# Causal attention with routed experts on one core: the expert units are laid out over fewer of the attention slots

## The reference

```
xn  = layernorm(x)
out = x + attention(xn) + experts(xn)

attention: q, k, v = xn@Wq+bq, xn@Wk+bk, xn@Wv+bv     16 heads of 16
           softmax(q k^T / 4, causal) v, then @ Wo + bo
experts:   16 routed experts, 4 per token, inner width 176, softmax gate, weights renormalised
           y = sum of weight * (silu(x Wg) * (x Wu)) Wd
           and a shared expert of inner width 352 for every token
```

## Time and profile before

| | |
|---|---|
| median of 3 runs | 1187.9 us (1186.93 to 1193.66) |
| the profiled execution's own time | 1184.47 us |
| its span, first to last instruction | 1182.9 us |
| mean granted TensorE clock | 0.939 of full |
| busy: PE, DVE, ACT, POOL | 989.0, 855.2, 652.1, 586.8 us |
| slots 0 to 319 (first to last exponential's start) | 204.1 to 1138.0 us |
| from there to the end | 44.9 us |

### The profile page before, as it was taken

The page is one execution under the profiler, slowest core; times in us unless marked ns, Lnnn a source line. Parts: engine busy times, 40 slices in busy tenths (PEclk is TensorE's granted clock), DMA queues, the critical chain, the costliest instruction groups (busy, mean ns, idle before and its releaser), DMA issues.

```text
span 1182.9 us, 26391 instructions
## 1 busy us (share of the span) xinstructions
PE 989.0 (84%) x8630; PEld 519.4 (44%) x8630; DVE 855.2 (72%) x1787; ACT 652.1 (55%) x1219; POOL 586.8 (50%) x527
## 2 busy tenths in 40 slices
PE   2877515999989899989998999999889998999980
PEld 1454302544444444544444445444444554444450
DVE  5888687888888877667876676777777767786320
ACT  4777500554545455466665654666656556766630
POOL 6433207777761004356665653566556535667521
PEclk9888755999999999999998999999999999999995
DMA  6998726223233313544454443644444445444348
GB/s 168 282 294 279 238 64 179 70 71 99 71 109 104 92 55 78 91 83 91 87 96 83 83 83 66 106 91 90 91 86 88 86 74 98 67 78 71 67 68 152
DMA packets 102284, 128.01 MB, mean 108 GB/s; under 512 B 25513, under 2 KB 86202, under 8 KB 101650
## 3 DMA queue, kind: packets, MB, share of 16 engines
q0 software_dynamic: 41632, 60.79, 28.6%
q1 hardware_dynamic: 60530, 65.59, 18.8%
HBM read 72.16 MB, written 57.82 MB: 110 GB/s over the span
## 4 chain that ended last, share of the span: by engine, by line
PE 55%; DVE 13%; issue 7%; ACT 4%; DMA 3%; SPq 1%; POOL 0%; ACTq 0%; DVEq 0%; POOLq 0%
PE gup L1191 12%; PE pvp L1131 11%; PE outs L1218 9%; DVE part L1285 7%; PE smp L1087 6%; PE turn L1203 5%; PE stp L1112 4%; PE outs L1138 4%; PE turn L1167 3%; DVE sg L1324 2%; PE smp L1070 1%; ACT XC L1440 1%; DVE hf L1329 1%; ACT th L1429 1%; DVE probs L1357 1%
## 5 line engine op out<-in xcount | busy, mean ns | idle before, releaser
L1423 ACT ACTIVATE probs<-stp 128x1024 f32<-128x1024 f32 (+1 forms) x320 | 300.4, 939 | 276.0 <-PE stp L1112 271.2
L1285 DVE TENSOR_REDUCE part<-smp 128x2 f32<-128x256 f32 (+2 forms) x372 | 345.8, 951 | 45.3 <-PE smp L1070 28.2
L1191 PE MATMUL gup<-gu_w,XC 128*128 (+1 forms) x1248 | 226.4, 318 | 11.3 <-DVE hf L1329 10.8
L934 POOL DMA_INDIRECT XG<-xrow_d,slots x144 | 146.5, 1017 | 131.6 <-DMA out<-Y 86.3
L941 POOL DMA_INDIRECT out<-Y,slots x72 | 118.1, 1640 | 136.1 <-ACT Y L1456 113.9
L1218 PE MATMUL outs<-dn_w,h 88*128 (+1 forms) x1248 | 181.0, 276 | 0.1
L941 POOL DMA_INDIRECT acc_d<-Y,slots x72 | 118.8, 1650 | 118.6 <-ACT Y L1456 104.9
L1131 PE MATMUL pvp<-probs,Vs 128*32 128x512 f32 (+3 forms) x1536 | 165.5, 503 | 3.3 <-DVE probs L1357 2.7
L1324 DVE SCALAR_TENSOR_TENSOR sg<-th,gup 128x176 f32<-128x176 f32 x208 | 69.8, 336 | 119.9 <-ACT th L1429 117.4
L1087 PE MATMUL smp<-Ks,Qs 48*128 48x128 f16 (+2 forms) x744 | 112.3, 340 | 45.7 <-DVE part L1285 26.9
L923 POOL DMA_INDIRECT slot_d<-entry,slot_i x128 | 128.5, 1004 | 42.8 <-issue 42.8
(11 more groups left out here) (168 smaller groups left out, 1099.2 us busy)
## 6 DMA issues: line engine op xcount, KB each, us to landing
rb<-rsum_d SPq DMA_DIRECT2D x64, 128.0 KB
Ks<-k_d SPq DMA_DIRECT2D x96, 64.0 KB
Qs<-q_d SPq DMA_DIRECT2D x96, 64.0 KB
v_d<-V SPq DMA_DIRECT2D x8, 544.0 KB, 4.6
Vs<-v_d SPq DMA_DIRECT2D x16, 272.0 KB, 3.3
acc_d<-YA SPq DMA_DIRECT2D x1, 4224.0 KB, 16.3
X<-L_attn_x POOLq DMA_DIRECT2D x8, 512.0 KB, 4.7
xrow_d<-XR SPq DMA_DIRECT2D x8, 512.0 KB, 5.0
```

What stands on the lines that cost most here:

```text
L934: pool.indirect_dma_start(XG[:, q].rearrange("p a c t -> p (a c t)"), None, s.xrow_d, bass.IndirectOffsetOnAxis(ap=slots[:, r, 0:1], axis= ...
L1191: last = pe.matmul(gup[:, 0:2 * I], XC[:, x % 2, a, h], weights_of(s.gu_w, e, b, h, slice(0, 2 * I)), start=n == 0, stop=n == 5)
L1285: last = dve.tensor_reduce(part[:, g % 2, k0 // CH, :, j, t], banks[:, :, col:col + w], AX.X, ALU.max)
L1423: act.activation(to, of, ACT.Exp, scale=float(DK) ** -0.5 / QS ** 2).then_inc(exp_done, 1)
```

## The change

`SPARE` goes from 4 to 18: the planner divides the same work by 302 slots instead of 316.

```diff
-        LAG, SPARE = 2, 4
+        LAG, SPARE = 2, 18
         FIRST, SECOND = spread_units()
         second_slot = {v: g * SLOTS + n for (g, n), v in SECOND.items()}
```

## The result

The changed kernel takes 1208.7 us (median of 6 runs, 1205.02 to 1212.81) against 1185.5 us (6 runs) of the kernel before: ratio 1.0193, 95% interval 1.0172 to 1.0215, or +23 us (+20 to +25). The forecast was 1201, +13. The direction and the range held; the loss is nearly twice the forecast's. The profiled execution has a span of 1203.4 us, 20.5 more than the one before; it was the fastest of its six.

The account below looks back on a forecast made before the run. PE was taken to bound the kernel, busy 989.0 us. +33 us in the first 296 slots less 20 at the end gave +13 on a median of 1187.9, so 1201 us, range 1186 to 1211.

Parts of the forecast that it names:

- Part 1: End of the kernel: last scatter and merges stay behind the last down product after slot 319; cost and gain 0.
- Rival 4: End of the kernel: the merges start early, beside the attention, some 25 us of the end go, 1176; chance 0.03.
- Part 2: Slot 296 to the start of slot 319, emptied of units: from 64.4 to 40.7 us at full clock, gain 24.
- Part 3: Emptied stretch from slot 296: PE about half busy, clock falls to 1.2 GHz for a good part, +4 (0 to +12).
- The swing: Emptied stretch: PE's share rises again at half clock and the next window was faster, so +4, a third of 12.
- rival 1: Stretch without units stays at 1.2 GHz, costing 12 us there: +21 in all, or 1209; chance 0.18.
- Part 4: First 296 slots take the 35 us of moved PE work, 2 us of it hidden: +33 (bounds +18 and +37).
- rivals 2 and 3: Slots 0 to 295: PE's idles hide half the moved work (1186, chance 0.13) or nearly all (1176, chance 0.11).

Follow-up runs that it names:

- experiment 3: Changed kernel with the last unit's down product and result issued behind its second half: ratio to before 1.0157; kernel before with them in slot 316: 0.9988.
- experiment 1: Kernel before (SPARE 4) with the last 14 of the 144 routed units left out altogether: ratio 0.9897, 12 us faster.

## Why the forecast came out as it did, step by step

- **Part 1, the end does not move by the layout: right.** POOL waited 49.2 us for the last unit, and the tail was 43.5 us against 44.9. From the last down product to the end it was 41.8 us (from 1161.60) against 42.8; the forecast said 43. Rival 4 is out, and experiment 3 shows that this order is the reason: with the last unit early the tail is 29.4 us.
- **Part 2, the emptied stretch at full clock: right.** The forecast said 40.7 us; with the clock held up (0.96) it took 41.5. One count was off: 16 second halves leave slots 296 to 319, not 15. A slip without effect: in group 14 DVE has 13.8 us free (58.0 less 44.2), not 14 or more.
- **Part 3, the clock: mechanism right, size off.** The term was +4; it measured 6.4 (47.9 less 41.5). PE's share did rise at the lower clock, to 26.3 of 38.0 us in the last group, but the clock stayed at 0.54. The swing that I drew from the earlier trace rows did not come; the row from 176 us there, low clock at 58% busy, was the better guide. This is half of rival 1: its condition held, but its price of 12 was too high. By the Trainium skill's rule on swinging ("TensorE: Matmul & The Clock Gate", "A second HAM failure mode: psum-queue depth-cycling") the term was +6, near the measured one. The trace shows little swinging, though: in windows of 3 us from 1119 to 1140 the clock was 0.96 once (from 1134) and 0.50 to 0.61 in all others, and from 1140 to 1160 it was 0.50.
- **Part 4, the price ahead of slot 296: right in kind, too small.** The term was +33, with a bound of +37; the profile has +38.8. PE's busy time there rose by 841.8 less 804.7 = 37.1 us and its idle from 64.8 to 66.5. So nothing of the moved work hid in the idles, the 2 us that I had let hide included; rivals 2 and 3 are out. Of the 37.1 us, 1.1 is the second half that I missed, and up to 2.7 are not moved work at all but a lower clock: slots 0 to 295 lost 12.6 us of full clock to its falls instead of 9.9. What the moved work itself takes is then near the 35 us. Part 4 had no term for the clock.
- **The sum.** Forecast +33 less 20 = +13. Profile +38.8 less 16.5, 1.4 and 0.4 = +20.5. Runs +23. The two mis-sized terms were Part 4 (5.8 us) and Part 3 (2.4 us), and both erred towards the small side. The measured 1208.7 us is rival 1's number, 1209, but that is luck: the clock in the emptied stretch was half of what rival 1 charged, and the rest lies ahead of slot 296.
- **What the forecast did not have.** Its Part 4 prices moved work by its amount alone. The ratios of SPARE 1 and SPARE 11 show that this is not enough: a step the other way costs 13 us instead of gaining 2 to 5, and half of the way costs three quarters of the loss. In the profiles the first 296 slots are off by several us (SPARE 1: 9.6 us longer with some 7 us less work), with different falls of the clock and different waits; which of the two is the cause is open. That the amounts fit so well for 18 may be partly luck, and the 35 us between the changed kernel and experiment 1 may contain such a share too.

## What to carry to other kernels

Before work is moved away from the end so that the end comes earlier, look which instruction releases the last transfer: here the last unit's result stood behind the loop in program order, and no layout could move it. Where one engine is busy for nine tenths of the time, ask whether what is taken from a looser stretch is paid in full in the dense ones, as the 35 us were here, and whether the loose stretch gives back as much as it lost: here it gave back 16.5 us for the 35, and 6.4 us of what is missing was its clock. Before a large transfer is moved beside other work, look whether small transfers are due then that an engine waits for. And a price per slot did not carry from one value of a layout's constant to the next here: 1 and 11 both came out slower than it said, so each value has to be measured.

## What the runs showed of the hardware that was not expected

- PE at 0.54 of full clock for 38 us while it was busy for 26.3 of them; with products added that nobody reads the stretch went from 47.9 to 41.5 us and the kernel from 1.0193 to 1.0101.
- Beside merges of 1024 KB, which kept the DMA engines busy (share 0.91 to 1.02, 207 to 213 GB/s), a write of 16 KB took 9.4 us instead of 1.4.
- A wait of PE of 2 us was followed by 6 us at a mean clock of 0.72 in one place and 0.50 in another, and in a third, of 2.29 us, the clock stayed at 1.00.
